# A second pair of PSUM banks for the row scores of causal attention, and the causal mask of the column scores moved to GpSimd

## The reference, cut to what matters

```python
q = concatenate([q_c, rope(q_e)]); k = concatenate([k_c, rope(k_e)])   # (8 batches, 16 heads, 512, 8)
scores = einsum('bhqd,bhkd->bhqk', q, k) / sqrt(8)
scores = where(tril(ones(512, 512)), scores, -inf)                     # a query sees the keys up to itself
att = softmax(scores, axis=-1)
y = einsum('bhqk,bhkd->bhqd', att, v).reshape(8, 512, 128)
causal = y @ Wc
```

## Time and profile before

| | us |
|---|---|
| median of 3 runs (4016.85 to 4025.20) | 4020.49 |
| the profiled execution | 4023.4 |
| its span | 4021.5 |
| PE busy / DVE / ACT / POOL in the span | 3620.6 / 3032.2 / 2850.0 / 2423.1 |
| causal attention, about 80 to 560 us: length | 480 |
| PE busy / DVE / ACT / POOL in it | 391.4 / 265.7 / 215.4 / 59.1 |

### The profile page before, as it was taken

One profiled execution on the slowest core, in us unless ns is written; L12 is line 12 of the kernel. 1 busy time (PEld: TensorE's weight loads), 2 busy tenths in 40 slices (PEclk: granted clock), 3 DMA queues, 4 the chain that ended last, 5 costly groups with the idle time before them and its releaser, 6 DMA issues.

```text
span 4021.5 us, 98070 instructions
## 1 busy us (share of the span) xinstructions
PE 3620.6 (90%) x31846; PEld 2751.9 (68%) x32224; DVE 3032.2 (75%) x4780; ACT 2850.0 (71%) x6080; POOL 2423.1 (60%) x2185
## 2 busy tenths in 40 slices
PE   5888868999989999979999889999899999799998
PEld 3444436777667777657777567776677776577776
DVE  4665538888678888678887688886688886788876
ACT  2444447888668888668887578886588886688875
POOL 1111117777457777467776477775577774677763
PEclk9998979999989999989999999999899999899999
DMA  3222210000100000100000100001000001000002
GB/s 123 71 66 77 61 45 2 0 0 0 28 2 1 0 0 0 28 2 1 0 0 1 29 2 0 0 0 28 2 2 0 0 0 29 2 1 0 0 1 70
DMA packets 59737, 67.80 MB, mean 17 GB/s; under 512 B 12006, under 2 KB 40164, under 8 KB 58468
## 3 DMA queue, kind: packets, MB, share of 16 engines
q1 hardware_dynamic: 59492, 64.64, 5.6%
HBM read 46.27 MB, written 18.35 MB: 16 GB/s over the span
## 4 chain that ended last, share of the span: by engine, by line
PE 30%; issue 23%; ACT 21%; DVE 21%; ACTq 1%; DVEq 1%; POOL 1%; DMA 0%; SPq 0%; POOLq 0%
PE bank L387 26%; ACT sb_area L772 10%; DVE sb_ssq L1280 9%; DVE sb_smax L1291 5%; ACT sb_area L911 5%; DVE sb_area L1132 3%; ACT sb_lnb L923 2%; ACT sb_lnb L920 2%; PE bank L607 2%; PE bank L636 1%; POOL sb_area L1505 1%; DVE sb_area L1268 1%; DVE sb_area L1294 0%; PE bank L665 0%; ACT sb_wqk_hi L772 0%
## 5 line engine op out<-in xcount | busy, mean ns | idle before, releaser
L772 ACT ACTIVATE sb_area<-bank 128x512 f32<-128x512 f32 (+3 forms) x2533 | 1359.0, 577 | 268.7 <-PE bank L387 205.7
L1268 DVE TENSOR_TENSOR sb_area<-bank,sb_rots 128x1024 f32<-128x1024 f32 x768 | 939.4, 1225 | 398.4 <-ACT sb_area L911 397.3
L387 PE MATMUL bank<-sb_area 128*64 128x64 f32 (+5 forms) x17616 | 1113.7, 273 | 71.8 <-issue 57.6
L1480 POOL TENSOR_TENSOR sb_area<-sb_area,sb_rn 128x512 f32<-128x512 f32 x768 | 784.8, 1043 | 609.5 <-ACT sb_rn L927 609.5
L1466 POOL TENSOR_TENSOR sb_area<-sb_area 128x512 f32<-128x512 f32 x768 | 967.8, 1278 | 91.6 <-DVE sb_area L1268 87.9
L387 PEld LDWEIGHTS bank<-sb_area 128*64 128x64 f32 (+4 forms) x17616 | 767.3, 144 | 186.6 <-issue 133.0
L387 PE MATMUL bank<-sb_wqk_hi,sb_xwin 128*128 128x512 f32 x1536 | 725.6, 474 | 58.5 <-DVE sb_xwin L1248 48.1
L387 PE MATMUL bank<-sb_area,sb_wvo 128*128 128x256 f32 x3072 | 728.5, 381 | 3.1 <-DVE sb_xT L1326 3.1
L387 PEld LDWEIGHTS bank<-sb_area,sb_wvo 128*128 128x128 f32 x3072 | 556.3, 191 | 77.2 <-issue 12.8
L607 PE MATMUL bank<-sb_ident,sb_area 128*128 128x128 f32 x3072 | 491.9, 284 | 38.3 <-ACT sb_area L772 32.5
L607 PEld LDWEIGHTS bank<-sb_ident,sb_area 128*128 128x128 f32 x3072 | 356.5, 143 | 230.9 <-issue 160.2
(11 more groups left out here) (113 smaller groups left out, 4153.2 us busy)
## 6 DMA issues: line engine op xcount, KB each, us to landing
qk_rows<-sb_p SPq DMA_DIRECT2D x52, 256.0 KB, 4.0
sb_wqk_hi<-qk_rows SPq DMA_DIRECT2D x32, 256.0 KB, 2.9
sb_wqk_lo<-qk_rows SPq DMA_DIRECT2D x32, 256.0 KB, 2.7
sb_area<-in_Wqkv SPq DMA_DIRECT2D x7, 1024.0 KB, 5.9
sb_area<-in_WvT SPq DMA_DIRECT2D x7, 512.0 KB, 7.6
sb_wo_bd<-in_Wo SPq DMA_DIRECT2D x14, 256.0 KB, 8.6
sb_area<-in_x SPq DMA_DIRECT2D x4, 512.0 KB, 6.3
sb_area<-in_x SPq DMA_DIRECT2D x8, 256.0 KB, 3.1
```

The source lines that it names most:

```text
L387: return nc.tensor.matmul(o, a, b, start=start, stop=stop, skip_group_check=True)
L772: return nc.scalar.activation(o, i, ACT.Copy)
L1268: tt_(t12[:, c % 2, :, :].rearrange("p u (h d) -> p u h d", h=8), src, bc(rots[:, tt, s, :, :], [P, 2, 8, D], 2), ALU.mult).then_inc(S["ro ...
L1480: pt_(qn[:, c, :].rearrange("p (h d) -> p h d", h=8), qsum[:, c % 2, :].rearrange("p (h d) -> p h d", h=8), r, ALU.mult).then_inc(S["qn"], 1)
```

## The change

1. The row scores have two pairs of banks, 0 and 1, and 2 and 3, that are used in turn. All side work and the transposition of the maxima take their turn in the same two pairs: `turn` numbers the writers, and a writer waits until the writer before the last has been read (`rows_read` for readers on DVE, `rows_read_act` on ACT). The two projections of a side stand together in one turn.
2. The column scores have three banks (4 to 6) for 12 outputs in rotation, and no mask: their mask matmuls are gone. A pair now waits for the first exponential of the pair before it.
3. GpSimd writes zeros into the four diagonal blocks of a group's exponentials (`causal_part`, one affine_select of 128 x 4 x 128 for each kt). The exponentials have two buffers.
4. The weighing stands in one place, in the next slot after unit 0, for all kt, into bank 7, and waits for GpSimd. The transposition of the maxima moves behind it.
5. Side work moves: both key projections to k = 2 (so k = 3 has none, k = 1 has the output and both query projections); DVE's rope stages move with them.

```diff
-        et0, et1, et2 = take(4, T), take(4, T - P), take(4, T - P)
+        et0, et1, et2 = take(2, 4, T), take(2, 4, T - P), take(2, 4, T - P)
...
-        m_at = {}
+        by_act = ("v", "perm")
+        turn, ordinal, count = {}, {}, {"rows_read": 0, "rows_read_act": 0}
+        order = []
         for s in range(FIRST, LAST + 1):
-            for name, there in ((("max", s - 1), slot(s - 1)),
-                                ((("v", s // 4), ("out", (s - 9) // 4), ("rope", (s + 6) // 4, 1), ("rope", (s + 5) // 4, 2))[s % 4],
-                                 valid((s // 4, (s - 9) // 4, (s + 6) // 4, (s + 5) // 4)[s % 4])),
-                                ((("perm", (s - 4) // 4, 0), ("rope", (s + 7) // 4, 0), ("perm", (s - 6) // 4, 1),
-                                  ("rope", (s + 5) // 4, 3))[s % 4],
-                                 valid(((s - 4) // 4, (s + 7) // 4, (s - 6) // 4, (s + 5) // 4)[s % 4]))):
+            k = s % 4
+            for op, there in ((("unit", s, 0), slot(s)), (("max", s - 1), slot(s - 1)), (("unit", s, 1), slot(s)),
+                              (("unit", s, 2), slot(s)),
+                              (("v", s // 4), k == 0 and valid(s // 4)), (("out", (s - 9) // 4), k == 1 and valid((s - 9) // 4)),
+                              (("rope", (s + 6) // 4, 1), k == 2 and valid((s + 6) // 4)),
+                              (("unit", s, 3), slot(s)), (("unit", s, 4), slot(s)),
+                              (("perm", (s - 4) // 4, 0), k == 0 and valid((s - 4) // 4)),
+                              (("rope", (s + 7) // 4, 0), k == 1 and valid((s + 7) // 4)),
+                              (("perm", (s - 6) // 4, 1), k == 2 and valid((s - 6) // 4)),
+                              (("unit", s, 5), slot(s)), (("unit", s, 6), slot(s)), (("unit", s, 7), slot(s))):
                 if there:
-                    m_at[name] = len(m_at)
+                    reader = "rows_read_act" if op[0] in by_act else "rows_read"
+                    turn[op] = len(order)
+                    order.append((reader, count[reader] + 1))
+                    count[reader] += 1
+                    ordinal[op] = count[reader]
+
+        def rows_banks(*op):
+            first = 2 * (turn[op] % 2)
+            return banks[:, first:first + 2, :]
...
-            def bank_m(*op):
-                need(pe, "m_free", m_at[op])
-                return ps[7]
-
-            def project_causal(a, i):
-                mm(bank_m("rope", a, i), wcomb[:, i, :], xT[:, a * T:(a + 1) * T]).then_inc(S["c_proj"], 1)
+            def free_banks(*op):
+                if turn[op] >= 2:
+                    reader, reads = order[turn[op] - 2]
+                    pe.wait_ge(S[reader], reads)
+                return rows_banks(*op)
+
+            def project_causal(a, side):
+                o = free_banks("rope", a, side)
+                for i in range(2):
+                    mm(o[:, i, :], wcomb[:, 2 * side + i, :], xT[:, a * T:(a + 1) * T]).then_inc(S["c_proj"], 1)
 
             def causal_values(a):
-                o = bank_m("v", a)
+                o = free_banks("v", a)
...
             def rows_of_scores(n, u):
                 hg, x, qt = n % 4, u // 4, u % 4
-                need(pe, "c_max", 8 * n + u)
+                o = free_banks("unit", n, u)
                 if u == 0:
                     pe.wait_ge(S["qm_ready"], 2 * n + 2)
                     pe.wait_ge(S[f"stack_k{hg}"], 16 * (n // 4 + 1))
                 keys, queries = (qt + 1) * P, slice(qt * P, (qt + 1) * P)
                 low, high = slice(0, 64), slice(64, P)
                 for g, rows in ((0, low), (1, high)):
-                    mm(ps[g][:, 0:keys], qm[rows, n % 4, x, queries], stack_k[rows, hg, 0:keys], True, False)
+                    mm(o[:, g, 0:keys], qm[rows, n % 4, x, queries], stack_k[rows, hg, 0:keys], True, False)
...
             def columns_of_scores(n, p):
                 hg, T_, x = n % 4, p // 2, p % 2
-                need(pe, "c_exp", 12 * n + 2 * p - 2)
+                need(pe, "c_exp", 12 * n + 2 * p - 1)
                 if p == 0:
                     pe.wait_ge(S[f"mrow{hg}"], 2 * 16 * (n // 4 + 1))
-                b0 = ps[2 + 2 * p % 4], ps[3 + 2 * p % 4]
+                o = ps[4 + 2 * p % 3], ps[4 + (2 * p + 1) % 3]
                 low, high = slice(0, 64), slice(64, P)
                 blocks = (((0, 0),), ((1, 0),), ((2, 0), (3, 2 * P)))[T_]
                 for kt, c0 in blocks:
                     for g, rows in ((0, low), (1, high)):
-                        mm(b0[g][:, c0:c0 + T - kt * P], stack_k[rows, hg, kt * P:(kt + 1) * P], qm[rows, n % 4, x, kt * P:T], c0 == 0, False)
-                for kt, c0 in blocks:
-                    for g, rows in ((0, low), (1, high)):
-                        mm(b0[g][:, c0:c0 + P], tri[rows, :], identb[rows, :], False, False)
-                    for g, rows in ((0, low), (1, high)):
-                        m = mm(b0[g][:, c0:c0 + P], tri2[rows, :], identb2[rows, :], False, True)
+                        m = mm(o[g][:, c0:c0 + T - kt * P], stack_k[rows, hg, kt * P:(kt + 1) * P], qm[rows, n % 4, x, kt * P:T],
+                               c0 == 0, True)
                         if kt == blocks[-1][0]:
                             m.then_inc(S["c_s2"], 1)
 
-            def weigh_causal(n, kt):
+            def weigh_causal(n):
                 a, hg = n // 4, n % 4
-                pe.wait_ge(S["c_exp"], 12 * n + (4, 8, 12, 12)[kt])
-                if kt == 0 and hg % 2 == 0:
-                    pe.wait_ge(S["m_free"], m_at["v", a] + 1)
+                pe.wait_ge(S["c_exp"], 12 * n + 12)
+                if hg % 2 == 0:
+                    pe.wait_ge(S["rows_read_act"], ordinal["v", a])
                     need(pe, "c_yraw", 2 * a + hg // 2)
-                e, c0 = ((et0, 0), (et1, 0), (et2, 0), (et2, 2 * P))[kt]
-                for r in range(4):
-                    m = mm(ps[6][32 * r:32 * r + 32, kt * P:T], v32[:, a % 2, (kt * 4 + r) * 2 + hg // 2, hg % 2, :],
-                           e[:, r, c0:c0 + T - kt * P], hg % 2 == 0 and kt == 0, hg % 2 == 1 and kt == 3)
-                    if kt != 2:
-                        m.then_inc(S["c_pv"], 1)
+                for kt in range(TT):
+                    pe.wait_ge(S["c_sel"], 4 * n + kt + 1)
+                    e, c0 = ((et0, 0), (et1, 0), (et2, 0), (et2, 2 * P))[kt]
+                    for r in range(4):
+                        m = mm(ps[7][32 * r:32 * r + 32, kt * P:T], v32[:, a % 2, (kt * 4 + r) * 2 + hg // 2, hg % 2, :],
+                               e[:, n % 2, r, c0:c0 + T - kt * P], hg % 2 == 0 and kt == 0, hg % 2 == 1 and kt == 3)
+                        if kt == 3:
+                            m.then_inc(S["c_pv"], 1)
...
                 pair(0)
+                unit(0)
+                if slot(n2 - 1):
+                    weigh_causal(n2 - 1)
                 if slot(n1 - 1):
                     turn_max(n1 - 1)
-                unit(0)
-                weigh(n2 - 1, 2)
-                weigh(n2 - 1, 3)
                 pair(1)
                 unit(1)
+                unit(2)
+                pair(2)
                 if k == 0 and valid(s // 4):
                     causal_values(s // 4)
                 if k == 1 and valid((s - 9) // 4):
                     causal_out((s - 9) // 4)
                 if k == 2 and valid((s + 6) // 4):
                     project_causal((s + 6) // 4, 1)
-                if k == 3 and valid((s + 5) // 4):
-                    project_causal((s + 5) // 4, 2)
-                pair(2)
-                unit(2)
-                weigh(n2, 0)
                 unit(3)
                 pair(3)
+                unit(4)
                 if k == 0 and valid((s - 4) // 4):
                     move_sums((s - 4) // 4, 0)
                 if k == 1 and valid((s + 7) // 4):
                     project_causal((s + 7) // 4, 0)
                 if k == 2 and valid((s - 6) // 4):
                     move_sums((s - 6) // 4, 1)
-                if k == 3 and valid((s + 5) // 4):
-                    project_causal((s + 5) // 4, 3)
-                unit(4)
+                unit(5)
                 pair(4)
-                unit(5)
-                weigh(n2, 1)
+                unit(6)
                 pair(5)
...
-                need(act, "c_pv", 12 * (n - 1) + 4 * T_ + 4)
+                need(act, "c_pv", 4 * (n - 1))
                 for g in range(2):
                     act.wait_ge(S["c_s2"], 12 * n + 2 * p + g + 1)
-                    nc.scalar.activation((et0, et1, et2)[T_][:, 2 * g + x, :], ps[2 + (2 * p + g) % 4][:, 0:w], ACT.Exp)                        .then_inc(S["c_exp"], 1)
+                    nc.scalar.activation((et0, et1, et2)[T_][:, n % 2, 2 * g + x, :], ps[4 + (2 * p + g) % 3][:, 0:w], ACT.Exp)\
+                        .then_inc(S["c_exp"], 1)
...
+                    turned(6, 1, 0)
+                    turned(6, 1, 1)
...
```

(16 more changed lines are left out.)

121 lines of the change are left out of this document (54 added, 67 removed).

## The result

The changed kernel takes 3947.2 us (3946.3 to 3947.6, 4 runs) against 4018.7 before: ratio 0.982, with an interval of 0.980 to 0.984. The forecast was 3942 in 3907 to 3990. 71.5 us went; from the span of one profiled execution to the other it is 76.

The account below looks back on a forecast made before the run. PE was near its limit (11.4 of 14.13 us per slot) but waited. Slots of 12.5 against 14.92 us give 72 us, plus 7 at the edges; 4023.4 - 79 = 3944, forecast 3942 us, range 3907 to 3990.

Parts of the forecast that it names:

- The bound and the two waits: PE near its limit yet waiting; unit 7 (1.08 us) and the transposition (1.29) stand for maxima; 2.4 us per slot go.
- Masks, 0.9 us a slot "counts in full": Column-score mask matmuls removed from PE save 0.9 us per slot, range 0.7 to 1.4, in full since PE is near its limit.
- Weighing in one piece, 0.25: Merging the weighing's pieces on PE saves 0.25 us per slot, between nothing and 0.5.
- The walk: Stepping through one slot with recorded durations to count new waits; gave 11.85 us per slot at full clock.
- New waits, 1.5: PE's new waits at units 2, 4, 5, 6 and pairs 0, 3, 5 sum to 1.5 us per slot.
- Rival (a): Less gained: side work and scores share a turn, waits chain to 2.7 to 3.3 us; 3962 to 3996 us; chance 0.24.
- GpSimd: Four selections per group at 1.04 us each stay hidden behind PE's other work, with 0.3 us to spare.
- X: Time of one GpSimd selection, taken as 1.04 us; PE stands 1.3 + 2X - 3.7 us per slot for it.
- The casts: DVE casts slow while GpSimd works: about 3 more hit at 0.77 us, 0.6 per slot, 0.05 on the path.
- The DMA loop: From unit 0 through the maxima's DMAs to the next keys, 9.3 to 10.7 us, below which no slot can go.
- The clock: PE's granted clock keeps the same loss as before, so a slot takes 12.5 us against 14.92.
- The edges: Outside the 30 full slots: first two slots gain 7 us; the phase's end adds 2 and saves 2.

Follow-up runs that it names:

- split_pe_masks: Changed kernel with column masks back on PE, no GpSimd selections, and the weighing in three places: 3915.4 us, 0.974 of the kernel before.
- after_pe_masks: Changed kernel with the column masks back on PE, no GpSimd selections nor waits for them: 3954.2 us, 0.982 of the kernel before.
- the filler run: Changed kernel plus 24 useless matmuls behind the output projection in each slot k = 1: 3933.8 us, 0.978 of the kernel before.
- the split: Changed kernel with the weighing in three places again, masks still on GpSimd: 3920.5 us, 0.975 of the kernel before.
- the late division: DVE's k = 1 division behind the maximum of unit 2, weighing in three places: 3911.0 us with GpSimd's masks, 3900.0 with masks on PE.
- the doubled selection: Changed kernel with each GpSimd selection made twice: 3961.0 us, 0.985 of the kernel before.

## Why the prediction was right

**The bound and the two waits**: right. Both named waits come from the single pair of banks, and they go; with one pair the rest of the change is a loss. By the prediction's own sum the banks were worth little net, 2.4 us of waiting less 1.5 of new waiting. Without the masks' move and the single piece (split_pe_masks) a slot falls by 2.9 us, from 14.92 to 11.98. There PE waits for DVE 0.6 us a slot, and the clock goes from 0.93 to 0.97. So this part was priced too low, and it is what carries the result.

**Masks, 0.9 us a slot "counts in full"**: this step failed. The size was near: 0.68 us where both kernels run at the same clock (after_pe_masks). What failed is that it counts in full: over all slots it measures 0.12, since in the slots k = 1 and k = 3 the kernel without the masks runs at a lower clock. For k = 1 the filler run shows that work put into PE's wait brings the clock back. For k = 3 it is not shown why the clock falls without the masks: in the two slots shown PE is idle for 1.9 us without them and 2.1 with them. In the split, at an equal clock, the kernel without the masks on PE is 5 us slower, and with the late division some 11; there the weighings wait for the selections (in the row at 151.79 above by 0.48 us). On the kernel before, it is 20 us slower, with the clock at 0.82.

**Weighing in one piece, 0.25**: failed, with the wrong sign. It costs 27 us, 1.05 us a slot (12.98 against 11.93). The walk did see DVE idle for 2.5 us behind it, but priced that at 0.2 for unit 2. The piece itself did get cheaper, 2.44 us against 0.87 + 1.16 + 0.87 = 2.9 in three: two of them are in the earlier trace rows, and kt 1, from this start to the next at 423.39 less 0.06 of mask, is this row of the kernel before:

```profile
422.46 1.00 PE L387 MATMUL bank<-sb_area 64*128 64x128 bf16 x10
```

But the piece stands ahead of the transposition, and DVE and the clock paid for it.

**New waits, 1.5**: near in sum and wrong in place. In the change PE waits for DVE and ACT 1.7 us a slot. The walk spread this over all slots and missed the division of the slots k = 1, which waits for the output projection and holds the maximum behind it: 1.75 us of PE at once and 0.92 behind it, and with the clock a slot of 16.0 us. Rival (a), waits that chain through the shared turn, is what happened there. At a clock of 1.00 the slots k = 0 took 11.74 and the slots k = 2 12.06 us in the mean, near the 11.85 that the walk gives for a mean slot.

**GpSimd**: hidden in the change, as forecast, but for 12.8 us in 300 of the weight loads; X is 0.65 and not 1.04, and the doubled selection landed in the range of the formula. The Trainium skill, in "GPSIMD Engine Reference" ("Elementwise — side-by-side cycle accounting"), would have given 0.77 by its best rate, nearer than the row that was taken; the measured time lies under it. **The casts**: they got cheaper (mean 549 ns against 807, 80 to 440 us), so the added work of GpSimd did not collide with them as priced. They were cheaper too without any selections (689 ns in after_pe_masks), so a part of it is that they stand elsewhere in the slot. **The DMA loop** of 9.3 to 10.7 us: the slots k = 3 of the split take 10.1, which lies in that range, but PE has no wait for a DMA in its list, so no run shows the loop to bind. **Rival (a)'s range**: its slots of 13.7 to 14.4 us give 3977 to 3998 by the prediction's own sum, where it says 3962 to 3996; the result lies outside both.

**The clock**, taken as the same loss: it became worse (0.88 in place of 0.93), which is why the slot is 12.98 and not 12.5. **The edges**: 16 us and not 7. So 72 + 7 forecast against 60 + 16 measured. The mechanism was right in its main part, and the closeness of the sum is partly luck: what stays in split_pe_masks gave 105 us, the single piece took back 27 and the masks off PE 5, where the forecast had both as gains. These shares depend on the order: with the single piece in place, taking the masks off PE gains 0 to 7 us.

## What to carry to other kernels

A second pair of banks, so that writer and reader take turns, was worth more here than trimming the writer's work; look for the engine that is near its limit and still waits, and name the two longest waits. Before work is merged or taken away on PE, ask what the others do meanwhile: a long piece ahead of a small step that another engine needs costs that engine the whole piece, and PE that stands idle may lose its clock. When several engines walk a fixed order, look for an instruction that waits for an output ahead of one whose input has long been there: moving it one place was worth 10 us in one kernel here and 15 in another.

## What the runs showed of the hardware

Adding 192 useless matmuls made the kernel 13 us faster. The granted clock went with where PE waits, and not simply with how busy it is: PE is busy for 0.86 of the stretch between the rests both in the change and in after_pe_masks, at a clock of 0.88 and 0.94. The lowest clock, 0.63, came with one pair, where PE is idle in almost a third of the stretch; it was 0.82 where masks were taken from a PE that waits, and 0.97 to 0.99 in the kernels with the weighing in three pieces. In the slot shown PE fell from the higher level (2.4 GHz) to the lower (1.2) behind two waits of 1.75 and 0.92 us, and stayed at it for about 10 us. The Trainium skill, "TensorE: Matmul & The Clock Gate" ("Part 1: The HAM clock gate"), ties the lower level to low activity of the engine; the filler run agrees. Selection of 4 x 128 elements by 128 partitions on GpSimd: 0.65 us in the mean, most of them 0.61 to 0.64, against 1.04 for a product of 512 elements.
